# Key and query products of a chunk from float16 parts, and the gate's multiplication on VectorE

## The chip, the cores and the metric

The kernel runs on one core of a Trainium2 chip. Its engines are TensorE (PE in the rows; its weight loads stand apart as PEld), VectorE (DVE), ScalarE (ACT), GpSimd (POOL) and SyncE (SP, which issues the DMAs). Each works through its own queue of instructions in order, and they wait for one another by semaphores. The metric is the time on the device in microseconds (us), the median of several runs.

## The reference

A macaron block over x of shape (8, 512, 256): half a gated feed-forward network (width 768, quantised weights), a gated linear attention with the delta rule (16 heads of 128), and the same half network again. What matters here is the attention of one head:

```python
q = silu(conv(x @ Wq)); k = silu(conv(x @ Wk)) * D ** (-0.5); v = silu(conv(x @ Wv))
alpha = sigmoid(x @ Wa + ba); beta = sigmoid(x @ Wb + bb)
def step(St, inp):                       # one token
    err = St @ k_ - v_
    Sn = a_ * St - b_ * err[..., None] * k_[..., None, :]
    return Sn, Sn @ q_
o = layernorm(o) * ln_w + ln_b
g = sigmoid(x @ Wg)
return (o * g) @ Wo
```

conv is a causal convolution of four taps in each channel.

## The kernel before

**Tiling.** The 16 heads are taken in four groups of U = 4, and for each group the 8 sequences one after the other: 32 pairs of group and sequence (SEQ). A sequence of 512 tokens is cut into NC = 4 chunks of C = 128. So there are 128 chunks (STEPS), numbered t = 4n + c for pair n and chunk c. The token recurrence of a chunk is solved in matrix form: two products of the chunk, keys by keys (gram_k) and keys by queries (gram_q), each times a matrix of decays; the inverse of a triangular matrix, built in six levels (level_a and level_b on TensorE, each followed by a copy on VectorE or ScalarE); a solution and its correction; and the update of the state.

**Storage.** The rows of k, q and v (kb, qb, vb) and of the gate (gb) are float32 in SBUF, channels on partitions, twice for alternate pairs n. Weights and normed inputs are pairs of float16, high and low part, and the products of such pairs are made of three matmuls (high by high, high by low, low by high). The two chunk products take float32 operands straight from kb and qb: one call for each of four heads, which stands in the trace as two instructions.

**Where the projections lie.** While chunk t is solved, the projections for the next pair of group and sequence are made: project(t', j) with t' = 4n + i makes head j of k, q, v or gate for i = 0, 1, 2, 3, so each chunk's time holds one of the four. For i = 0, 1, 2 ScalarE starts the convolution (acc, L2219), VectorE does three taps for each head (tap, L1684) and ScalarE the silu (L2229). For i = 3 ScalarE applies tanh (gate, L2243), and there are no taps. Two PSUM banks take the projections in turn, and project(t', j) waits until the bank's last reader is done (tile_done).

**The output of a chunk.** statistics and aggregated (VectorE), root (POOL), normed (ScalarE), out_turned (TensorE), affine into oa (ScalarE), gated on POOL (oa times gb), high (ScalarE, the float16 part), low (POOL, the rest), output (TensorE, 12 matmuls) and the addition to the stream (VectorE). The gate is tanh plus 1 (the half is put in later): POOL adds the 1 in `one`, four instructions of 128x512 for each pair n.

**Order.** Each engine's block has a function step(s) that holds its order by hand for one chunk's time, a loop over it for the chunks of the middle, and orders written out line by line before and after. SyncE loads the decay and cumulative rows of each chunk and, at a change of the head group, the group's five weight pairs (load_pairs); the output weights wo16 have two places in SBUF, taken alternately.

**Two inputs in SBUF.** Of VectorE's instructions in the loop only the scan in decays (L1584) reads both inputs from SBUF. The others have at least one in PSUM.

## Time and profile before

| | |
|---|---|
| time, median of 3 runs | 2388.95 us (2388.93 to 2389.35) |
| the profiled execution's own time | 2389.32 us |
| its span, first to last instruction | 2387.6 us |
| mean granted TensorE clock | 0.996 |
| busy: PE, DVE, ACT, POOL | 98%, 85%, 76%, 76% |
| DMA | 43 GB/s on average |

Busy time of an engine is the time in which at least one of its instructions is in flight. TensorE's matmuls are pipelined: the duration of one holds the way through the array, in which the next has already started, so what an instruction costs a full TensorE is the distance between starts. For VectorE in a dense row, too, the next start lies about 0.08 us before the last end. Times in the timelines are microseconds from the span's start.

### The profile page before, as it was taken

The page shows a single profiled execution, that of the slowest core. Times are in us where ns is not written, and L with a number is a line of the kernel's source. Part 1 is how long each engine was busy: PE and PEld are TensorE (multiplying, and loading weights), DVE is VectorE, ACT ScalarE, POOL GpSimd, SP SyncE. Part 2 cuts the span into 40 slices and gives each one's busy share as a digit, 9 for nine tenths or more (in the row PEclk, how much of TensorE's full clock was granted, in tenths as well). Part 3 has the DMA queues.
Part 4 walks back from the last instruction along what each step waited for, and adds up shares of the span by engine and source line. Part 5 has one row for each costly group of instructions (what it writes and reads, how often), then busy time and mean ns, then how long its engine had stood idle before and what let it go on. Part 6 is the DMA issues. An engine that isn't in the chain of part 4 may idle for free. (4 is left out here: it accounts for less than half of the span.)

```text
span 2387.6 us, 64265 instructions
## 1 busy us (share of the span) xinstructions
PE 2338.4 (98%) x24496; PEld 1818.2 (76%) x24496; DVE 2023.1 (85%) x4282; ACT 1813.6 (76%) x3572; POOL 1809.2 (76%) x1936
## 2 busy tenths in 40 slices
PE   5999999999999999999999999999999999999998
PEld 2555778888888888788888887888888887887765
DVE  8788988888888888888889888888888888899653
ACT  3876777777777787777777877777777777788664
POOL 4774777877777777777777778777777777788775
PEclk8999999999999999999999999999999999999999
DMA  5450111111021111111121111111211121111001
GB/s 140 130 168 34 34 33 25 32 33 33 24 68 41 30 26 33 33 33 33 46 59 33 30 27 33 33 30 27 68 42 27 29 53 33 33 33 28 17 28 45
DMA packets 72832, 103.59 MB, mean 43 GB/s; under 512 B 21456, under 2 KB 33744, under 8 KB 72400
## 3 DMA queue, kind: packets, MB, share of 16 engines
q1 hardware_dynamic: 72528, 99.48, 16.3%
q8 instruction: 197, 3.23, 0.5%
q14 instruction: 107, 0.88, 0.1%
HBM read 85.69 MB, written 13.77 MB: 42 GB/s over the span
## 5 line engine op out<-in xcount | busy, mean ns | idle before, releaser
L1684 DVE SCALAR_TENSOR_TENSOR k_rows<-bank,k_prm,k_rows 128x511 f32<-128x511 f32 (+2 forms) x1152 | 842.5, 736 | 9.6 <-ACT k_rows L2219 8.8
L2970 PE MATMUL bank<-k_z,k_kqv 128*128 128x512 f16 x2304 | 597.4, 379 | 2.6 <-DVE k_rows L1684 2.5
L2281 ACT ACTIVATE k_wide<-bank 128x512 f16<-128x512 f32 x640 | 382.9, 599 | 200.3 <-PE bank L2803 184.5
L1613 DVE TENSOR_TENSOR k_y<-bank,k_masks 128x256 f16<-128x256 f32 x768 | 317.7, 414 | 120.5 <-PE bank L2789 116.6
L2219 ACT ACTIVATE k_rows<-bank,k_prm 128x512 f32<-128x512 f32 x384 | 299.4, 780 | 130.8 <-PE bank L2970 130.6
L2970 PEld LDWEIGHTS bank<-k_z,k_kqv 128*128 128x128 f16 x2304 | 197.5, 98 | 127.5 <-issue 4.7
L1205 POOL TENSOR_TENSOR k_diag<-k_ident,k_bcol 128x512 f32<-128x512 f32 x128 | 132.9, 1039 | 190.7 <-DVE a_prod L1584 190.6
L2803 PE MATMUL bank<-k_wide,k_y 128*128 128x64 f16 x3072 | 271.1, 192 | 0.0
L2789 PEld LDWEIGHTS bank<-k_wide 128*128 128x128 f16 x3072 | 169.0, 98 | 91.9 <-ACT k_wide L2281 1.8
L2801 PE MATMUL bank<-k_y,k_wide 128*128 128x64 f16 x2560 | 235.8, 193 | 2.7 <-DVE k_y L1613 0.8
L2803 PEld LDWEIGHTS bank<-k_wide,k_y 128*128 128x128 f16 x3072 | 207.0, 98 | 32.6
L2229 ACT ACTIVATE k_rows<-k_rows 128x512 f32<-128x512 f32 x384 | 230.3, 629 | 1.8 <-DVE k_rows L1684 1.8
L2801 PEld LDWEIGHTS bank<-k_y,k_wide 128*128 128x128 f16 x2560 | 196.8, 98 | 42.2 <-DVE k_y L1613 16.4
L1219 POOL TENSOR_TENSOR k_wide<-k_solve,k_ident 128x512 f16<-128x512 f32 x128 | 163.4, 1277 | 83.0 <-DVE k_solve L1593 78.6
L1301 POOL TENSOR_SCALAR k_rows<-k_rows 128x512 f32<-128x512 f32 x128 | 218.4, 1706 | 0.0
L2789 PE MATMUL bank<-k_wide 128*128 128x64 f16 x3072 | 215.1, 193 | 1.0 <-ACT k_wide L2281 0.7
L2970 PE MATMUL bank<-k_z,k_gate 128*128 128x512 f16 x768 | 201.4, 379 | 0.0
L2306 ACT ACTIVATE k_narrow<-bank,a_shift,a_rstd 128x128 f32<-128x128 f32 x512 | 191.7, 462 | 0.1
L2941 PE MATMUL bank<-k_wo,k_solve 128*128 128x256 f16 x1536 | 188.6, 273 | 0.0
L2901 PE MATMUL bank<-k_solve,k_wide 128*128 128x128 f32 x1024 | 184.9, 277 | 0.0
L1584 DVE TENSOR_TENSOR_SCAN a_prod<-a_decay,k_diag 128x516 f32<-128x516 f32 x128 | 180.3, 1408 | 0.5 <-ACT k_wide L2256 0.5
L1310 POOL TENSOR_TENSOR k_narrow<-k_narrow,k_rows 128x512 f32<-128x512 f32 x128 | 163.4, 1276 | 19.4 <-ACT k_narrow L2315 19.4
(158 smaller groups left out, 5870.2 us busy)
## 6 DMA issues: line engine op xcount, KB each, us to landing
a_decay<-decay_rows SPq DMA_DIRECT2D x128, 258.0 KB, 3.6
k_solve<-cumulative_rows SPq DMA_DIRECT2D x96, 258.0 KB, 3.6
weight_pairs<-k_wide SPq DMA_DIRECT2D x15, 512.0 KB, 2.9
k_kqv<-weight_pairs SPq DMA_DIRECT2D x9, 512.0 KB, 5.0
stream<-in_L_attn_x SPq DMA_DIRECT2D x8, 512.0 KB, 7.6
out<-stream SPq DMA_DIRECT2D x8, 512.0 KB, 2.9
k_rows<-in_L_attn_Wk SPq DMA_DIRECT2D x4, 512.0 KB, 4.7
k_rows<-in_L_attn_Wq SPq DMA_DIRECT2D x4, 512.0 KB, 5.2
```

The costliest lines, as they stand in the source:

```text
L1301: nc.gpsimd.tensor_scalar(gb[:, n % 2, j], gb[:, n % 2, j], 1.0, None, ALU.add).then_inc(m["pool_one"], 1)
L1613: nc.vector.tensor_tensor(even(y16[:, j], mb), bank[LEV[par]][:, 0:U * C // 2].rearrange("p (u b m) -> p u b m", u=U, m=mb), masks[:, j].r ...
L1684: nc.vector.scalar_tensor_tensor(out=dst[:, d:S], in0=bank[PJ[j % 2]][:, 0:S - d], scalar=prm[:, i, U * (n // B) + j, TAPS - 1 - d:TAPS - ...
L2219: nc.scalar.activation((kb, qb, vb)[i][:, n % 2, j], bank[PJ[j % 2]][:, :], ACT.Identity, bias=prm[:, i, h, TAPS:], scale=prm[:, i, h, TAP ...
L2229: nc.scalar.activation(dst, dst, ACT.Silu).then_inc(m[f"act_silu{j}"], 1)
L2281: nc.scalar.activation(both, bank[LEV[par]][:, :].rearrange("p (two b m) -> p two b m", two=2, m=mb), ACT.Copy).then_inc(m[f"act_lev{par}" ...
L2306: ins = nc.scalar.activation(on[:, u], bank[OUT][:, u * D:(u + 1) * D], ACT.Identity, bias=shift[:, u:u + 1], scale=rstd[:, u:u + 1])
L2789: mm = pe.matmul(at_half(LEV[par], 0, u), am16[:, par, u], halves(t16[par][:, u], mb, 0), start=True, stop=True)
L2801: pe.matmul(at_half(LEV[par], 0, u), tt16[par][:, u], halves(y16[:, j, u], mb, 0), start=True, stop=True)
L2803: mm = pe.matmul(at_half(LEV[par], half, u), y16[:, j, u], halves(tt16[par][:, u], mb, 1), start=True, stop=True)
L2941: mm = pe.matmul(bank[SUM][:, 0:H], o[:, u], wo16[:, group % WO_SLOTS, wh, u], start=(u == 0 and wh == 0 and o is oh), stop=(u == U - 1 an ...
L2970: mm = pe.matmul(bank[PJ[j % 2]][:, :], wt, z16[:, zh, k, cols], start=(x == 0), stop=(x == 5))
```

## The change

- A new tile k16 and a new tile q16 hold the float16 high part and low part of the keys and of the queries of one chunk. ScalarE makes the high parts (key_high, query_high: copies to float16), POOL the low parts (key_low, query_low: the row minus its high part, to float16).
- gram_k and gram_q make each head's product of three float16 matmuls of the parts (pair_products) instead of a float32 one.
- gated moves from POOL to VectorE and becomes one scalar_tensor_tensor, (gb + 1) * oa. `one` is gone.
- wo16 has one place instead of two. Its load at a change of the group comes three chunk times later and waits until the output of the last group's last chunk is done.
- pool_shift and pool_root (with their like) are one semaphore each.
- In the last block the second half of the last sequence is added to the stream by VectorE and stored by a DMA of its own. The down product of that block signals its first half early.
- step(s) of TensorE, VectorE, ScalarE and POOL is written in another order, and so are the written-out parts ahead of and behind the loops. Each engine still does all the same other work.

```diff
+    k16 = sb("k16", [P, 2, U, C], F16); q16 = sb("q16", [P, 2, U, C], F16)
...
@@ SyncE
-            group, kind = divmod(s - NC * (B - 1) + 2, NC * B)
+            group, place = divmod(s - NC * (B - 1) + 2, NC * B)
             group += 1
-            if kind >= KINDS or not 0 < group < HG:
+            kind = KINDS - 1 if place == WO_PLACE else place
+            if not 0 < group < HG or kind >= KINDS or place == KINDS - 1:
                 return
...
-                need(sp, m["pe_wo"], NC * B * (group - WO_SLOTS + 1))
+                need(sp, m["pe_wo"], NC * B * group)
...
@@ POOL
-        def one(t, j):
...
-            pool.wait_ge(m[f"act_gate{j}"], n + 1)
-            nc.gpsimd.tensor_scalar(gb[:, n % 2, j], gb[:, n % 2, j], 1.0, None, ALU.add).then_inc(m["pool_one"], 1)
...
-            nc.gpsimd.tensor_tensor(oa[:, :, :], oa[:, :, :], gb[:, n % 2, :, c * C:(c + 1) * C],
-                                    ALU.mult).then_inc(m["pool_og"], 1)
+        def key_low(t):
...
+            pool.wait_ge(m["act_kh"], t + 1)
+            nc.gpsimd.tensor_tensor(k16[:, 1], kb[:, n % 2, :, c * C:(c + 1) * C], k16[:, 0],
+                                    ALU.subtract).then_inc(m["pool_kl"], 1)
...
+            pool.wait_ge(m["act_qh"], t + 1)
+            nc.gpsimd.tensor_tensor(q16[:, 1], qb[:, n % 2, :, c * C:(c + 1) * C], q16[:, 0],
+                                    ALU.subtract).then_inc(m["pool_ql"], 1)
...
+            system16(s)
+            first_inverse(s)
+            query_low(s)
+            scaled_q(s - 1)
+            scaled_k(s - 1)
+            root(s - 2)
+            low(s - 3)
+            strengths(s + 1)
             system_low(s)
+            key_low(s + 1)
             state(s - 1)
...
@@ VectorE
+        def gated(t):
...
+            dve.wait_ge(m["act_oa"], t + 1)
+            if c == 0:
+                for j in range(U):
+                    dve.wait_ge(m[f"act_gate{j}"], n + 1)
+            nc.vector.scalar_tensor_tensor(out=oa[:, :, :], in0=gb[:, n % 2, :, c * C:(c + 1) * C], scalar=1.0,
+                                           in1=oa[:, :, :], op0=ALU.add, op1=ALU.mult).then_inc(m["dve_og"], 1)
...
+            level(s - 1, 3)
+            tap(s + 2, 0, 2)
+            gated(s - 3)
+            tap(s + 2, 0, 3)
+            tap(s + 2, 1, 1)
+            statistics(s - 2)
+            level(s - 1, 4)
...
+            level(s, 1)
+            tap(s + 2, 2, 2)
+            tap(s + 2, 3, 1)
+            tap(s + 2, 2, 3)
+            output(s - 3)
+            tap(s + 2, 3, 2)
+            decays(s + 1)
+            tap(s + 2, 3, 3)
+            residual(s - 1)
+            level(s, 2)
+            system(s + 1)
+            corrected(s - 1)
+            tap(s + 3, 0, 1)
...
+                nc.vector.tensor_tensor(rows, rows, scaled[:, 2:4], ALU.add).then_inc(f["dve_last"], 1)
...
@@ ScalarE
+        def key_high(t):
...
+            need(act, m["pe_gram0"], t)
+            need(act, m["pe_gram1"], t)
+            nc.scalar.activation(k16[:, 0], kb[:, n % 2, :, c * C:(c + 1) * C], ACT.Copy).then_inc(m["act_kh"], 1)
...
+            need(act, m["pe_gram1"], t)
+            nc.scalar.activation(q16[:, 0], qb[:, n % 2, :, c * C:(c + 1) * C], ACT.Copy).then_inc(m["act_qh"], 1)
...
+            level(s, 4)
+            key_high(s + 2)
+            level(s + 1, 0)
+            normed(s - 1)
+            acc(s + 3, 3)
...
@@ TensorE
+        def pair_products(dst, a, b, u):
+
+            pe.matmul(dst, a[:, 0, u], b[:, 0, u], start=True, stop=False)
+            pe.matmul(dst, a[:, 0, u], b[:, 1, u], start=False, stop=False)
+            return pe.matmul(dst, a[:, 1, u], b[:, 0, u], start=False, stop=True)
...
-                mm = pe.matmul(units(TURN)[:, u], kb[:, n % 2, u, cols], kb[:, n % 2, u, cols], start=True, stop=True)
+                mm = pair_products(units(TURN)[:, u], k16, k16, u)
...
-                mm = pe.matmul(units(TURN)[:, u], kb[:, n % 2, u, cols], qb[:, n % 2, u, cols], start=True, stop=True)
+                mm = pair_products(units(TURN)[:, u], k16, q16, u)
...
+            check_solution(s - 2)
+            project(s + 2, 0, 2)
+            gram_k(s)
+            project(s + 2, 1, 0)
+            correction(s - 2)
+            level_b(s - 1, 2)
...
```

## Rows read from the trace of the kernel before

**Rows 1.** The page: busy us of each engine, share of the span, instructions.

```profile
PE 2338.4 (98%) x24496; PEld 1818.2 (76%) x24496; DVE 2023.1 (85%) x4282; ACT 1813.6 (76%) x3572; POOL 1809.2 (76%) x1936
```

**Rows 2.** Stretches: us, busy PE, PEld, DVE, ACT, POOL (x instructions), clock, DMA.

```profile
1200.00:1600.00 400.00, 399.54 (x4456) 322.24 (x4455) 352.57 (x756) 314.72 (x630) 314.77 (x331) 1.00 0.13 34
...
1008.16:1057.71 49.55, 49.48 (x550) 40.16 (x549) 47.79 (x99) 38.56 (x76) 38.94 (x42) 1.00 0.14 34
1057.71:1071.65 13.94, 13.94 (x163) 10.94 (x163) 7.87 (x21) 11.36 (x24) 10.71 (x12) 1.00 0.08 20
```

**Rows 3.** Timeline of PE around one gram_k: start us, us in flight, engine, line.

```profile
1003.98 0.22 PE L2860 MATMUL bank<-k_solve,k_wide 128*128 128x128 f16 x1
...
1004.42 0.19 PE L2801 MATMUL bank<-k_y,k_wide 128*128 128x64 f16 x1
...
1004.66 1.14 PE L2739 MATMUL bank<-k_rows 128*128 128x128 f32 x8
1005.63 0.39 PE L2873 MATMUL bank<-k_solve,k_wide 128*128 128x128 f16 x4
1005.86 0.38 PE L2970 MATMUL bank<-k_z,k_kqv 128*128 128x512 f16 x1
```

**Rows 4.** Timeline of PE, the next gram_q.

```profile
1010.24 1.11 PE L2753 MATMUL bank<-k_rows 128*128 128x128 f32 x8
```

**Rows 5.** Timeline of DVE: the first tap of two successive pairs.

```profile
1008.16 0.75 DVE L1684 SCALAR_TENSOR_TENSOR k_rows<-bank,k_prm,k_rows 128x511 f32<-128x511 f32 x1 [0.27 <-ACT k_rows L2219]
...
1071.65 0.75 DVE L1684 SCALAR_TENSOR_TENSOR k_rows<-bank,k_prm,k_rows 128x511 f32<-128x511 f32 x1 [0.27 <-ACT k_rows L2219]
```

**Rows 6.** Timeline of DVE and of POOL around one scan, inside the taps.

```profile
1016.69 0.74 DVE L1684 SCALAR_TENSOR_TENSOR k_rows<-bank,k_prm,k_rows 128x511 f32<-128x511 f32 x1
1017.35 2.06 DVE L1584 TENSOR_TENSOR_SCAN a_prod<-a_decay,k_diag 128x516 f32<-128x516 f32 x1
...
1017.27 1.05 POOL L1280 TENSOR_TENSOR k_narrow<-k_narrow,k_solve 128x512 f32<-128x512 f32 x1
1018.29 2.40 POOL L1301 TENSOR_SCALAR k_rows<-k_rows 128x512 f32<-128x512 f32 x1
```

**Rows 7.** DVE: group of L1584 (busy us, mean ns), then lines with ns min/median/max.

```profile
L1584 DVE TENSOR_TENSOR_SCAN a_prod<-a_decay,k_diag 128x516 f32<-128x516 f32 x128 | 180.3, 1408 | 0.5 <-ACT k_wide L2256 0.5
...
L1584 DVE TENSOR_TENSOR_SCAN a_prod<-a_decay,k_diag x128: 1195/1223/2061, 180.9 to 2224.2; 128x516 f32<-128x516 f32 x128
...
L502 DVE SCALAR_TENSOR_TENSOR k_kqv<-k_rows,k_kqv x3: 1215/1216/1985, 63.5 to 82.0; 128x1024 f16<-128x1024 f32 x3
...
L515 DVE TENSOR_TENSOR k_rows<-k_rows x9: 693/693/1684, 7.7 to 49.0; 128x512 f32<-128x512 f32 x9
```

**Rows 8.** Groups of ACT and POOL by line.

```profile
L2323 ACT ACTIVATE k_solve<-k_narrow 128x512 f16<-128x512 f32 x128 | 79.2, 619 | 1.0 <-POOL k_narrow L1310 1.0
...
L1301 POOL TENSOR_SCALAR k_rows<-k_rows 128x512 f32<-128x512 f32 x128 | 218.4, 1706 | 0.0
L1310 POOL TENSOR_TENSOR k_narrow<-k_narrow,k_rows 128x512 f32<-128x512 f32 x128 | 163.4, 1276 | 19.4 <-ACT k_narrow L2315 19.4
L1241 POOL TENSOR_TENSOR k_wide<-k_solve,k_wide 128x512 f16<-128x512 f32 x128 | 148.3, 1159 | 0.1
```

**Rows 9.** Waits of the whole span: us in total, times, longest us.

```profile
POOL k_diag L1205 <- DVE a_prod L1584: 190.6, 93, 9.5
...
PEld bank L2860 <- ACT k_solve L2298: 25.6, 124, 0.5
...
PEld bank L2801 <- DVE k_y L1613: 16.4, 65, 0.7
```

**Rows 10.** Timeline of the end: the last scaling and the last additions.

```profile
2380.93 1.29 DVE L1770 TENSOR_TENSOR k_rows<-bank,k_rows 128x512 f32<-128x512 f32 x2 [4.49 <-PE bank L3078]
2381.70 2.48 POOL L1366 TENSOR_TENSOR stream<-stream,k_rows 128x512 f32<-128x512 f32 x2 [2.40 <-DVE k_rows L1770]
```

**Rows 11.** DMA issues: count, KB each, median us to landing.

```profile
k_wo<-weight_pairs SPq DMA_DIRECT2D x3, 512.0 KB, 5.6
```

More of the change, by code:

```diff
@@ L1894, in _ @@
         tap(4, 2, 2)
+        level(1, 5)
         level(2, 1)
@@ L2566, in _ @@
         level(5, 4)
+        key_high(7)
         level(6, 0)
-        acc(8, 2)
+        normed(4)
+        acc(8, 3)
+        right_side(5)
+        level(5, 5)
         kdecayed(6)
-        normed(4)
-        level(5, 5)
-        right_side(5)
         level(6, 1)
```

1878 lines of the change are left out of this document (1110 added, 768 removed).

## Prediction, made before the changed kernel was run

> **What bounds the kernel now.** I read the page's busy shares first: TensorE is busy for 98% of the span, VectorE for 85% [rows 1]. Such a share is an average, so the next view is the table of stretches. In 400 us of the middle TensorE has work in flight for 399.54 us at the full clock (1.00, the level of 2.4 GHz) [rows 2]. So in the loop every instruction taken from TensorE shortens the time, until another engine ends last. Of the 49 us that TensorE is idle in the span (2387.6 - 2338.4 [rows 1]) only some 2 us can lie in the loop (0.46 us in 400); the rest is at the two ends.
>
> The pattern repeats once for each pair of heads' group and sequence, which is four chunks: the first tap of a pair starts at 1008.16 and that of the next at 1071.65, so a period is 63.49 us [rows 5]. 32 periods are 2032 us of the 2387.6 us of span. Inside a period VectorE's load is uneven. The three chunks whose projections are keys, queries and values have 12 taps each, the fourth none. From the first tap to the last (1008.16 to 1057.71) VectorE is busy for 47.79 of 49.55 us; in the other 13.94 us it is busy for 7.87 us [rows 2]. I call the 49.55 us the tap stretch. In it VectorE is nearly as full as TensorE, which the share of 85% hides. This decides the case.
>
> **TensorE's part.** A float32 product of four heads is 8 instructions. The keys' product starts at 1004.66 and the next work at 1005.63: 0.97 us [rows 3]. The keys by queries are in flight for 1.11 us [rows 4]; less the same tail as above (1.14 - 0.97 = 0.17) that is 0.94 us. I take distances between starts, since the time in flight holds the way through the array, where the neighbour overlaps. The new product is 12 float16 matmuls of the same 128x128 shape. Eight such with changing weights take 1004.42 - 1003.98 = 0.44 us, or 55 ns each; four others 1005.86 - 1005.63 = 0.23 us, or 57 ns [rows 3]. Twelve are 0.66 to 0.69 us; I take 0.67. A chunk saves 0.97 + 0.94 - 2 * 0.67 = 0.57 us, a period 2.3 us, 128 chunks 73 us. The low parts accumulate in the same place of PSUM, as the projections do.
>
> One rule speaks against this. The Trainium skill, TensorE: Matmul & The Clock Gate, section Back-to-back issue gap, says that in a real stream of weight loads and matmuls the spacing at 128 columns is about 81 ns. By it twelve would take 0.97 us (estimate from the page), nothing would be saved, and the time would be 2389 us or more. The 55 ns here are from such a stream with a new weight load for each matmul, so the trace disagrees.
>
> **VectorE's part.** It gets one instruction of 128x512 for each chunk with both inputs in SBUF. The nearest rows: an addition of that shape takes 693 ns, and the same operation over 1024 elements 1216 ns [rows 7]. In a dense queue the next start comes 0.08 us before the end (a tap of 0.74 us starts at 1016.69, the scan at 1017.35 [rows 6]), so it costs 0.60 us in the queue; as bounds, 0.53 us (half of 1216 less 0.08) and 0.69.
>
> On top comes what the other input from SBUF does. The scan is the only such instruction now. Its median is 1223 ns and its longest 2061 [rows 7]: at 1017.35 it starts while POOL is in an instruction that ends at 1018.32, and lasts 0.84 us longer than the median; POOL's next lasts 2.40 us, 0.9 more than it would alone [rows 6]. They exclude each other. This happens to about one scan of four (mean 1408, median 1223 [rows 7]: 0.19 us a scan, 0.74 us a period). Most scans are spared because POOL sits waiting for that very scan: 190.6 us in all [rows 9]. In the new order POOL has strengths further from the scan it waits for, and gated comes two to three instructions after system, on whose end POOL starts system16 and first_inverse. So collisions are possible for three scans and three gated in a tap stretch. Bounds: none, or 0.84 us each, 5.0 us a period. If VectorE met POOL by chance, at its share of 38.94 in 49.55 us [rows 2] and half of some 1.1 us left, it would be 0.43 us each, 2.6 us. I take 1.3 us a period, 0.5 more than now, since POOL's long `one` is gone and its next idle time begins before system16.
>
> The Trainium skill, SBUF — State Buffer, has the rule for this: a VectorE instruction with two SBUF inputs and a GpSimd instruction that reads SBUF block each other for the whole instruction. The trace agrees with 2061 against 1223 ns.
>
> Now the sum for a tap stretch. TensorE's share of it falls by three chunks, 1.7 us, to 47.8 us. VectorE's real idle time is 49.55 - 47.79 = 1.76 us, plus the 0.08 us of overlap that each of its some eight short gaps would give back, 2.4 us. So its load is 47.1 us (with one collision), and with three gated 48.9, with 0.5 of further collisions 49.4. It exceeds TensorE's time by 1.6 us. TensorE can wait out some of that, since a level's copy may come late: I estimate 0.3 us, from PE's weight loads that already sit idle for VectorE's copy 65 times for 16.4 us in total, 0.25 us each [rows 9]. Give-back: 1.3 us a period. Net: 2.3 - 1.3 = 1.0 us a period, 32 us in all.
>
> **ScalarE and POOL.** ScalarE gets two copies of 0.62 us a chunk [rows 8], 3.7 us in the tap stretch: 38.56 + 3.7 = 42.3 of 47.8 us [rows 2], 88%. It costs nothing as long as level copies are not late behind them; if that cover is gone, a late copy costs TensorE what the queue holds, 0.6 us. For the solution's copy TensorE's weight loads wait already in 124 chunks, 0.2 us each [rows 9], so cover is thin. key_high waits for the previous chunk's gram_q; behind it in ScalarE's queue stand level, normed and acc, and for level waits TensorE. POOL loses 1.71 us (`one`) and 1.28 (gated) a chunk and gains two subtractions of 1.16 to 1.28 us [rows 8]: 0.4 to 0.7 us less. New chain: silu, high, low, product. At the first chunk of a pair it is 1.8 us longer (0.62 + 1.16) and gram_k waits on POOL; behind gram_k stand correction and level_b. gram_q now comes later in the step and has cover. gated waits for ScalarE's affine; behind it in VectorE's queue stand taps and level copies; affine is a good part of a chunk earlier in ScalarE's order, so nothing.
>
> **Queues and ends.** The output weights' load comes at three group changes on SP, behind the cumulative and decay loads of its step and ahead of the next ones, and waits for the last group's output. It lands in 5.6 us [rows 11], and the first output that needs it comes a chunk, 15 us, later: nothing; 17 us in all if that were wrong. Merged semaphores: nothing. At the end POOL's two additions run from 2381.70 to 2384.18 [rows 10]; with the second on VectorE, 0.6 us after its scaling that ends at 2382.22 and some 0.2 us earlier from the early signal, the last store starts about 1.7 us sooner. The rewritten beginning may move TensorE's idle time there by 4 us either way (estimate, a tenth of the 49 us).
>
> **Rivals.**
> - *TensorE alone bounds.* If the tap stretch has more slack than I count, all is kept: 2389 - 73 - 2 = 2314 us. For: TensorE's 399.54 of 400. Against: 47.79 of 49.55.
> - *Nearly all is given back*, by ScalarE's thin cover or collisions at the chance rate (2.6 us a period instead of 0.8: give-back 1.1 + 1.8 - 0.3 = 2.6 us, net -0.3; half of that excess gives +0.3 to +0.6 us): 2370 to 2390 us, 2380 in the middle.
> - *Slower: collisions on VectorE in the tap stretch.* With six of 0.5 us instead of one of 0.84 the give-back is 1.1 + 2.2 - 0.3 = 3.0 us against 2.3 saved: 32 * 0.7 = 22 us more, 2409 us. It decides from 2.3 us of collisions a period. For: the exclusion is in the trace. Against: POOL's idle share, and its own wait chains that fall together with VectorE's.
> - *The product isn't cheaper.* In the tap stretch TensorE starts 550 matmuls in 49.55 us, 90 ns apart on average [rows 2]. At 80 ns twelve cost what the float32 product costs and nothing is saved, 2389 us; at 90 ns each of 256 products costs 0.12 us more, 2420 us; 2400 in between. Against: 55 ns with changing weights [rows 3]. The Trainium skill's 81 ns (above) would be this rival.
>
> **How the numbers follow.** The profiled execution took 2389.32 us with a span of 2387.6, and the median of the runs is 2388.95, so they may be exchanged. Forecast: 2388.95 - 32 - 2 = 2355 us. Chances: forecast (2333 to 2370) 0.53; TensorE alone (2308 to 2332) 0.18; nearly all given back 0.15, half of it within 0.2%; slower by collisions 0.10; product not cheaper 0.04. A measurement of this kernel can tell about 0.2%, or 5 us, from no change. Faster: 0.53 + 0.18 + 0.07 = 0.78; within 0.2%: 0.08 + 0.02 = 0.10; slower 0.12. The range from 2314 to 2386 us leaves out the upper cases and a little of TensorE alone.
>
> **What would show it.** The products' distance in the timeline should be 0.66 to 0.69 us. The period should be 62.5 us. VectorE should be dense in the tap stretch, over 98%, with TensorE idle or its weight loads waiting for k_y, k_solve and k_rows of VectorE; if TensorE stays at 399.5 of 400 us and the period is 61.2, the first rival is right. The scan's and gated's medians against their longest durations give the collisions. Wrong would be: a f16 spacing over 70 ns, ScalarE as the named releaser of TensorE's new idle time, or a stall at the three group changes.

## The result, and the profile after

| | before | after |
|---|---|---|
| time, median of 4 runs each, side by side | 2389.15 us | 2408.41 us (2407.91 to 2408.60) |
| ratio | | 1.008, 95% interval 1.0067 to 1.0093 |
| span of the profiled execution | 2387.6 us | 2406.2 us |

The changed kernel is 19 us slower. The forecast was 2355 us with a range that ended at 2386, so both its sign and its range were wrong.

The page of after: busy us, share of the span and instructions; then the chain that ended last.

```profile
PE 2341.1 (97%) x25520; PEld 1730.8 (72%) x25520; DVE 2107.0 (88%) x4411; ACT 1967.4 (82%) x3828; POOL 1773.9 (74%) x1935
...
PE 67%; DVE 25%; issue 4%; POOL 2%; ACT 1%; DMA 0%; DVEq 0%; SPq 0%; POOLq 0%; ACTq 0%
```

TensorE's busy time is what it was [rows 1], 2341 against 2338 us, though it has 73 us less to do. A quarter of the chain now lies on VectorE.

Stretches of after, columns as in [rows 2]: first the middle, then the tap stretch of one period and its rest. To compare kernels I cut both at starts of taps: from a period's first tap to the start of its last one, and from there to the next period's first tap.

```profile
1200.00:1600.00 400.00, 396.49 (x4614) 300.52 (x4612) 360.58 (x764) 340.62 (x673) 301.48 (x325) 1.00 0.13 34
...
1016.02:1063.16 47.14, 46.63 (x534) 35.29 (x532) 46.82 (x98) 39.89 (x78) 37.98 (x41) 1.00 0.10 24
1063.16:1080.22 17.06, 17.06 (x212) 13.05 (x210) 11.33 (x28) 14.90 (x32) 10.41 (x12) 1.00 0.17 48
```

The kernel before, by the same cuts:

```profile
1008.16:1056.97 48.81, 48.74 (x544) 39.42 (x543) 47.05 (x98) 38.34 (x76) 38.28 (x41) 1.00 0.14 34
1056.97:1071.65 14.68, 14.68 (x170) 11.68 (x169) 8.61 (x22) 11.58 (x25) 11.38 (x13) 1.00 0.08 19
```

A period went from 63.49 to 47.14 + 17.06 = 64.20 us; 32 times 0.71 is 23 us, so the two ends gave some 4 us back. VectorE is busy for 46.82 of 47.14 us of the tap stretch, 99.3% (96.4% before). The rest of the period belongs to TensorE alone in both kernels. The granted clock is 1.00, the full one, in all of these stretches.

The product itself: TensorE in after, one gram_k and what follows it.

```profile
1030.25 0.22 PE L2900 MATMUL bank<-a_k 128*128 128x128 f16 x1
1030.30 0.22 PE L2901 MATMUL bank<-a_k 128*128 128x128 f16 x1
...
1030.92 0.59 PE L3154 MATMUL bank<-k_z,k_kqv 128*128 128x512 f16 x2
```

Twelve matmuls take 1030.92 - 1030.25 = 0.67 us. That was the forecast to the hundredth.

VectorE's instructions with two inputs in SBUF in after: ns min/median/max of the scan (L1597) and of gated (L1693), the groups' busy us and mean ns, and one gated beside POOL's queue.

```profile
L1597 DVE TENSOR_TENSOR_SCAN a_prod<-a_decay,k_diag x128: 1220/1416/2175, 204.4 to 2246.5; 128x516 f32<-128x516 f32 x128
...
L1597 DVE TENSOR_TENSOR_SCAN a_prod<-a_decay,k_diag 128x516 f32<-128x516 f32 x128 | 182.8, 1428 | 6.3 <-ACT k_wide L2327 6.1 <-POOL k_diag L1212 0.2
...
L1693 DVE SCALAR_TENSOR_TENSOR k_narrow<-k_rows,k_narrow x128: 658/956/1477, 263.1 to 2296.8; 128x512 f32<-128x512 f32 x128
...
L1693 DVE SCALAR_TENSOR_TENSOR k_narrow<-k_rows,k_narrow 128x512 f32<-128x512 f32 x128 | 115.6, 903 | 0.3 <-ACT k_narrow L2386 0.3
...
1034.33 0.98 DVE L1693 SCALAR_TENSOR_TENSOR k_narrow<-k_rows,k_narrow 128x512 f32<-128x512 f32 x1
...
1033.60 1.17 POOL L1238 TENSOR_TENSOR k_wide<-k_wide,k_mask0t 128x512 f16<-128x512 f16 x1
1034.72 1.61 POOL L1317 TENSOR_TENSOR a_q<-k_rows,a_q 128x512 f16<-128x512 f32 x1
```

gated starts at 1034.33 while POOL is in L1238 until 1034.77, and takes 0.98 us; with one input in PSUM it takes 0.68 (below). POOL's next takes 1.61 us. The median scan, 1223 ns before [rows 7], is 1416. Per period both together lose 4 * (903 - 676) + 4 * (1428 - 1223) ns = 1.7 us to POOL, against 0.74 before.

The waits of after (us in total, times, longest us):

```profile
PEld bank L2985 <- DVE k_y L1626: 55.4, 157, 1.1
PEld bank L2973 <- ACT k_wide L2352: 48.1, 155, 0.5
PEld bank L3034 <- issue: 43.8, 119, 0.4
PEld bank L3013 <- issue: 36.8, 86, 0.4
PEld bank L3057 <- DVE k_solve L1636: 23.3, 62, 0.7
PEld bank L3154 <- DVE k_rows L1708: 21.5, 52, 0.8
...
PE bank L3154 <- DVE k_rows L1708: 15.5, 41, 1.9
```

Of before there were two such lines in the loop, 25.6 and 16.4 us [rows 9]. Two of the new ones name no engine ("issue"): weight loads ahead of first_solution (L3034) and state_k (L3013). The weight loader idles while the array still holds earlier work, so a busy TensorE doesn't show it: in the kernel with the new order and the old work (below) TensorE is in flight for all but 0.14 us of a period, and the waits ahead of first_solution are 43 us all the same.

Where the order costs distances: `read` in before, then in after, then first_solution in after.

```profile
1023.34 0.47 PE L2900 MATMUL bank<-k_narrow 128*128 128x128 f32 x2
1023.64 0.39 PE L2901 MATMUL bank<-k_solve,k_wide 128*128 128x128 f32 x2
1023.86 0.39 PE L2900 MATMUL bank<-k_narrow 128*128 128x128 f32 x2
```

```profile
1033.03 0.46 PE L3084 MATMUL bank<-k_narrow 128*128 128x128 f32 x2
1033.32 0.39 PE L3085 MATMUL bank<-k_solve,k_wide 128*128 128x128 f32 x2
1033.54 0.39 PE L3084 MATMUL bank<-k_narrow 128*128 128x128 f32 x2
...
1034.22 0.47 PE L3084 MATMUL bank<-k_narrow 128*128 128x128 f32 x2
1034.53 0.39 PE L3085 MATMUL bank<-k_solve,k_wide 128*128 128x128 f32 x2
...
1027.62 0.59 PE L3154 MATMUL bank<-k_z,k_kqv 128*128 128x512 f16 x2
1028.16 0.38 PE L3034 MATMUL bank<-k_solve,k_wide 128*128 128x128 f16 x4
```

The first pair of float32 matmuls behind float16 work takes 0.30 us to the next start, the later ones 0.22. `read` is now in two halves with level_b between them, so that 0.08 us is paid twice a chunk. Two projection matmuls ahead of first_solution take 0.54 us; elsewhere two take 0.43 (1029.82 to 1030.25 in the same kernel).

### The profile page after: what moved, and what is told of

The parts are those of the page before. It is cut to its first block, busy times and chain, and to the rows that moved or that the text cites. A ratio compares the mean times of both kernels' runs of the same rounds, so it can differ in the third digit from the quotient of the medians.

```text
span 2406.2 us, 67114 instructions
## 1 busy us (share of the span) xinstructions
PE 2341.1 (97%) x25520; PEld 1730.8 (72%) x25520; DVE 2107.0 (88%) x4411; ACT 1967.4 (82%) x3828; POOL 1773.9 (74%) x1935
## 3 DMA queue, kind: packets, MB, share of 16 engines
q1 hardware_dynamic: 72544, 99.48, 16.4%
## 4 chain that ended last, share of the span: by engine, by line
PE 67%; DVE 25%; issue 4%; POOL 2%; ACT 1%; DMA 0%; DVEq 0%; SPq 0%; POOLq 0%; ACTq 0%
PE bank L3154 20%; DVE k_rows L1708 11%; PE bank L3125 5%; PE bank L3224 3%; PE bank L3084 3%; PE bank L3013 3%; DVE k_y L1626 3%; PE bank L2973 3%; PE bank L3085 2%; PE bank L2985 2%; PE bank L2987 2%; PE bank L828 2%; PE bank L3102 2%; PE bank L2900 2%; PE bank L3003 2%
## 5 line engine op out<-in xcount | busy, mean ns | idle before, releaser
L1708 DVE SCALAR_TENSOR_TENSOR k_rows<-bank,k_prm,k_rows 128x511 f32<-128x511 f32 (+2 forms) x1152 | 814.5, 732 | 1.2 <-ACT k_rows L2267 0.6
L3154 PE MATMUL bank<-k_z,k_kqv 128*128 128x512 f16 x2304 | 637.0, 380 | 18.8 <-DVE k_rows L1708 15.5
L2973 PEld LDWEIGHTS bank<-k_wide 128*128 128x128 f16 x3072 | 167.6, 97 | 129.8 <-ACT k_wide L2352 48.1
L3154 PEld LDWEIGHTS bank<-k_z,k_kqv 128*128 128x128 f16 x2304 | 179.3, 98 | 108.7 <-DVE k_rows L1708 21.5
L2985 PEld LDWEIGHTS bank<-k_y,k_wide 128*128 128x128 f16 x2560 | 188.7, 97 | 63.5 <-DVE k_y L1626 55.4
L3154 PE MATMUL bank<-k_z,k_gate 128*128 128x512 f16 x768 | 212.0, 379 | 0.1
L2987 PEld LDWEIGHTS bank<-k_wide,k_y 128*128 128x128 f16 x3072 | 197.8, 98 | 8.3
L1317 POOL TENSOR_TENSOR a_q<-k_rows,a_q 128x512 f16<-128x512 f32 x128 | 189.2, 1478 | 7.3 <-ACT a_q L2315 7.3
L3085 PE MATMUL bank<-k_solve,k_wide 128*128 128x128 f32 x1024 | 192.2, 280 | 0.0
L1597 DVE TENSOR_TENSOR_SCAN a_prod<-a_decay,k_diag 128x516 f32<-128x516 f32 x128 | 182.8, 1428 | 6.3 <-ACT k_wide L2327 6.1
L1238 POOL TENSOR_TENSOR k_wide<-k_wide,k_mask0t 128x512 f16<-128x512 f16 x128 | 163.4, 1276 | 10.1 <-PE bank L3057 0.3
L3084 PE MATMUL bank<-k_narrow 128*128 128x128 f32 x768 | 162.9, 294 | 0.2
```

The lines of the kernel that those rows point to most:

```text
L1708: nc.vector.scalar_tensor_tensor(out=dst[:, d:S], in0=bank[PJ[j % 2]][:, 0:S - d], scalar=prm[:, i, U * (n // B) + j, TAPS - 1 - d:TAPS - ...
L2973: mm = pe.matmul(at_half(LEV[par], 0, u), am16[:, par, u], halves(t16[par][:, u], mb, 0), start=True, stop=True)
L2985: pe.matmul(at_half(LEV[par], 0, u), tt16[par][:, u], halves(y16[:, j, u], mb, 0), start=True, stop=True)
L2987: mm = pe.matmul(at_half(LEV[par], half, u), y16[:, j, u], halves(tt16[par][:, u], mb, 1), start=True, stop=True)
L3084: pe.matmul(units(OUT)[:, u], qg[:, u], z[:, u], start=True, stop=False)
L3085: mm = pe.matmul(units(OUT)[:, u], mix[:, t % 2, u], wv[:, u], start=not c, stop=True)
```

## The experiments

Each ratio is against the kernel before on the same chip, whose median was 2389.2 to 2389.6 us in every group.

**The gate's instruction made short.**

```diff
-  ...scalar_tensor_tensor(out=oa[:, :, :], in0=gb[..., c * C:(c + 1) * C], scalar=1.0, in1=oa[:, :, :], ...)
+  ...scalar_tensor_tensor(out=oa[:, :, 0:4], in0=gb[..., c * C:c * C + 4], scalar=1.0, in1=oa[:, :, 0:4], ...)
```

> The changed kernel with gated on VectorE cut to 4 of 128 columns of each head (the rest of the gate's multiplication is left out). Theory A: VectorE's load binds the three chunks with taps (50.0 us from one first tap to where the next pair's would be), so without 0.50 us of work and about 0.28 us of collision for each of three chunks the stretch falls to TensorE's 47.5 us and the period from 64.2 to about 61.9 us: 2335 us. Theory B: the new order of TensorE's own queue leaves gaps whatever VectorE does: 2395 us or more. Theory C: ScalarE's two added copies are late: 2395 us or more.

2370.78 us (ratio 0.9922, 0.9907 to 0.9937): the instruction at full size costs 37.6 us more than the short one. None of the three theories had this: the first expected 2335 us, the others 2395 or more. VectorE is 99% busy in the tap stretch even so (45.44 of 45.95 us):

```profile
1002.72:1048.67 45.95, 45.68 (x534) 35.34 (x532) 45.44 (x98) 39.02 (x78) 36.61 (x41) 1.00 0.11 25
1048.67:1065.72 17.05, 17.05 (x212) 13.05 (x210) 10.80 (x27) 14.90 (x32) 9.93 (x12) 1.00 0.17 48
```

TensorE waits less for VectorE in it:

```profile
PEld bank L2985 <- DVE k_y L1626: 29.8, 98, 1.1
...
PEld bank L3154 <- DVE k_rows L1708: 6.6, 23, 0.8
```

In the changed kernel these two lines are 55.4 and 21.5 us. By distances from start to start, 0.5 of the 1.2 us a period that the full size costs lies between `update` and the projection behind it (L3154), whose PSUM bank VectorE's taps (L1708) still read; the rest is spread over several places.

**The products as before, in float32.**

```diff
-  mm = pair_products(units(TURN)[:, u], k16, k16, u)
+  mm = pe.matmul(units(TURN)[:, u], kb[..., cols], kb[..., cols], start=True, stop=True)
```

(and the same for keys by queries)

> The changed kernel with both chunk products made again from float32 rows; parts are still made and not used. TensorE gets 2.3 us a period back. Theory A: in the stretch with taps VectorE ends last, so only the fourth chunk pays its 0.57 us: 18 us more than the changed kernel, 2427 us. Theory B: TensorE's queue is the limit everywhere, gaps included: 73 us more, 2481 us.

2434.94 us (1.0190, 1.0175 to 1.0206): inside the changed kernel the float16 products bring 26.5 us, not the 73 of their distances. That is nearer to theory A's 2427 us than to theory B's 2481.

**The gate's second input from a bank at rest** in the three chunks with taps; the output of those chunks is multiplied with other data.

```diff
-  in1=oa[:, :, :]
+  in1=bank[PJ[0]][:, :]... if (s + 2) % NC < NC - 1 else oa[:, :, :]
```

> The changed kernel, but in chunks with taps gated takes its second input from a PSUM bank that lies still instead of from oa (the result is another). One input in SBUF: it should no longer collide with POOL. Theory A with collisions: 0.25 to 0.3 us less in each of three chunks, 0.06 us more for the PSUM input: about 0.6 us a period, 20 us less: 2388 us. Rival: collisions cost nothing, 2408 us.

2378.10 us (0.9954, 0.9939 to 0.9969). Same size, same place, one input in PSUM: 30.3 us back, half as much again as theory A's 20. gated falls from 903 to 676 ns:

```profile
L1694 DVE SCALAR_TENSOR_TENSOR k_narrow<-k_rows,bank 128x512 f32<-128x512 f32 x86 | 58.1, 676 | 0.0
L1694 DVE SCALAR_TENSOR_TENSOR k_narrow<-k_rows,k_narrow 128x512 f32<-128x512 f32 x42 | 32.4, 771 | 0.3 <-ACT k_narrow L2387 0.3
```

So most of the 37.6 us are collisions with POOL, not the instruction's own length. (Collisions are the cases in which an instruction of VectorE with both inputs in SBUF and one of POOL hold each other up.)

**The gate back on POOL** in the new order, with the 1 added on VectorE in the light chunk.

```diff
-  dve: scalar_tensor_tensor(oa, gb, 1.0, oa, ADD, MULT)
+  pool: gated_to(t - 3) ahead of system16: tensor_tensor(oa, oa, gb, MULT)
+  dve: one(n, j), tensor_scalar(gb[:, n % 2, j], ..., 1.0, ALU.add), in the chunk without taps
```

> Float16 products kept; the multiplication by the gate back on POOL (in its idle time ahead of system16), the added 1 on VectorE as four instructions of 128x512 in the chunk without taps. Theory A: VectorE's stretch is as in the kernel before, TensorE binds again with 2.3 us less: 2335 to 2350 us. Theory B or C: 2395 us or more. If POOL becomes late (1.28 us more a chunk) system16 comes later and TensorE's first_inverse waits: 2370 us.

2458.20 us (1.0289, 1.0272 to 1.0306). The last of the mechanisms that I had written, POOL late, is the one that the waits show, but I had priced it at 2370 us. POOL waits for ScalarE's affine ahead of system16 and is late with everything behind it:

```profile
POOL k_narrow L1312 <- ACT k_narrow L2413: 132.6, 117, 3.2
...
PEld bank L3084 <- DVE k_solve L1654: 89.8, 89, 2.2
```

It tells nothing of VectorE's load.

**One part or both in the order of before.** Three kernels: the gate on VectorE ahead of the level copy j = 3; the parts alone; both.

```diff
 level(t, j), VectorE
+            if j == 3:
+                gated_to(t - 2)
```

> The kernel before, in its own order, with one part of the change: the instruction (gb + 1) * oa on VectorE ahead of the level copy j = 3, and neither `one` nor the multiplication on POOL. The products stay float32. Nothing is left out of the computation. Theory L (VectorE's load and its collisions with POOL are what the change loses): VectorE gains four instructions of 0.60 us in a period, in the tap stretch three, where it has some 2 us of idle time; the previous runs put the gate's instruction at 38 us in the new order, where the stretch was fuller, because TensorE was shorter there. With TensorE still at its old length I expect 2389 to 2415 us, 2400 in the middle. Rival O (the new order of the engines costs, not VectorE): within 5 us of the kernel before, 2389 us.

2489.22 us (1.0420, 1.0404 to 1.0435). A miss, far above both ranges. gated takes 1147 ns on average here, against 659 at the least:

```profile
L1532 DVE SCALAR_TENSOR_TENSOR k_narrow<-k_rows,k_narrow 128x512 f32<-128x512 f32 x128 | 146.9, 1147 | 0.0
```

So some 62 of its 147 us are collisions, and the rest is its own length; the scan collides less than before (1226 ns on average). VectorE's busy time in the span grew by 2133.5 - 2023.1 = 110 us, the time by 100. The instruction stands ahead of a level copy in this order, and how much of the 100 us is that place wasn't told apart.

```diff
 order of before, with ScalarE and POOL (and VectorE's mixing moved, wo16 with one place)
+    high copies (act_kh, act_qh) ahead of level(t, 0) and kdecayed; key_low behind system_low, query_low behind first_inverse
+    gram_q behind level_a(t, 0); k_turned behind level_b(t, 0)
```

> The kernel before with the other part alone: both chunk products from float16 parts, with ScalarE's and POOL's instructions for them; the gating stays on POOL with `one`. The order is that of before, save for two products (keys by queries stands behind level_a of the level 0, the turned keys behind level_b of it), VectorE's mixing, and the place of the output weights. Nothing is left out. POOL now has everything of before and two subtractions of 1.2 us a chunk: its 314.77 us busy in 400 become 314.77 + 25.2 x 2.4 = 375, 94%. Theory L: TensorE's 73 us come through as far as POOL isn't late: 2320 to 2345 us. Rival P (POOL is late, as when the gating was put on it in the new order): 2370 us or more, with TensorE and VectorE waiting for POOL.

2672.78 us (1.1188, 1.1172 to 1.1205), rival P, and far beyond the 2370 that it named. POOL waits for ScalarE's query_high, and ScalarE for POOL's shift:

```profile
POOL a_q L1219 <- ACT a_q L2234: 273.0, 127, 4.9
...
ACT k_narrow L2365 <- POOL a_shift L1322: 231.3, 125, 2.3
```

> Both parts in the order of before: products from float16 parts, gating on VectorE, `one` gone. It is the whole change but for the rewritten order. Nothing is left out. Theory L (VectorE's load alone is the loss): the load is the same as in the changed kernel, so the time is too, 2400 to 2415 us. Rival O (the new order costs 1.2 us a period or more on TensorE, as the gaps that are left when the gate's instruction is made short suggest): 2408 less 38 = 2370 us, below 2380 at any rate.

2702.69 us (1.1312, 1.1293 to 1.1331), outside both ranges. These last two show only that the parts need places of their own in ScalarE's and POOL's queues, not what the order of the changed kernel costs. The next ones ask that from the other side.

**The new order with the old work**: float32 products and the gate's instruction on 4 columns, which is the first two edits together. It leaves out most of the gate, on POOL too, which has neither `one` nor the multiplication.

> The changed kernel with neither of its two effects: the products are float32 calls again (the parts are still made by ScalarE and POOL) and the gate's instruction on VectorE works on 4 of 128 columns, which leaves most of the gate out of the output. So TensorE has the work of the kernel before, VectorE too (but 0.1 us a chunk), and what differs is the order. If the effects add up: 2370.8 + (2434.9 - 2408.4) = 2397 us. Rival O (order costs of its own): 2397 us or more against 2389 for the kernel before. Theory L (the order costs nothing, its gaps are VectorE's): within 5 us of 2389.

2411.09 us (1.0091, 1.0076 to 1.0106). Rival O, and more than the 2397 us that the sum of the effects gives: TensorE's work is as before, and the kernel is 22 us slower.

**The same with the parts' four instructions on 4 columns.**

```diff
-  activation(k16[:, 0], kb[..., c * C:(c + 1) * C], ACT.Copy)
+  activation(k16[:, 0, :, 0:w], kb[..., c * C:c * C + w], ACT.Copy)    # w = C if t < 2 else 4
```

(and likewise query_high, key_low, query_low)

> The new order with the old work (float32 products, the gate's instruction on 4 of 128 columns), and now ScalarE's and POOL's four instructions for the parts on 4 of 128 columns too, from the third chunk on. Most of the gate is left out; the parts feed nothing. What is left of the change is the order of the queues. Theory T (the order of TensorE itself costs): the time stays at 2411 us, within 5. Rival S (the load of ScalarE and POOL, 2.4 and 4.8 us in a chunk's time of 16, makes copies late): back to 2389 to 2395 us.

2408.82 us (1.0081, 1.0066 to 1.0096). ScalarE's and POOL's added work is 2.3 us of the 22; 19.5 are left. They are not the price of the order by itself, since the gate's short instruction is still in VectorE's queue and takes far more than the 0.1 us that I had counted, 570 ns on average:

```profile
L1695 DVE SCALAR_TENSOR_TENSOR k_narrow<-k_rows,k_narrow x128: 142/417/1109, 264.4 to 2297.6; 128x16 f32<-128x16 f32 x128
```

That is 73 us of busy time which VectorE doesn't have in the kernel before, and no run takes it out. The period:

```profile
1018.13:1064.46 46.33, 46.19 (x514) 37.02 (x512) 45.48 (x98) 37.02 (x78) 31.17 (x41) 1.00 0.10 25
1064.46:1082.24 17.78, 17.78 (x200) 13.94 (x198) 11.67 (x27) 14.17 (x32) 8.06 (x12) 1.00 0.16 46
```

64.11 us, 0.62 more than before, with TensorE in flight for all but 0.14 us. VectorE is full in the tap stretch here too, 98%: the new order packs the same taps in 46.33 instead of 48.81 us. Three of the short instructions, 3 * (0.57 - 0.08) = 1.5 us, are among the 45.48.

**Two places of TensorE's order put back**, in the changed kernel and in the one with the old work.

```diff
-            read(s - 2, 0, U // 2)
-            level_b(s - 1, 3)
-            read(s - 2, U // 2, U)
+            read(s - 2, 0, U // 2)
+            read(s - 2, U // 2, U)
+            level_b(s - 1, 3)
...
-            first_solution(s - 1)
-            out_turned(s - 2)
+            out_turned(s - 2)
+            first_solution(s - 1)
```

> The changed kernel with two places of TensorE's order in the loop put as they were before: the two halves of `read` stand together again ahead of level_b(s - 1, 3), and out_turned stands ahead of first_solution. Nothing is left out. Reason: the kernel with the new order and the old work takes 2411 us against 2389, and in its rows the distances between starts are longer at read (0.6 us a period above that of its matmuls, 0.3 before), behind the first half of read (0.2) and ahead of first_solution (0.3; 43.8 us of weight loads that wait for nothing shown, none before). Theory O (these places are the cost of the order): 0.6 to 0.8 us a period come back as far as TensorE bounds; VectorE is full in the tap stretch, so about half of it: 2393 to 2403 us. Rival L (VectorE alone holds the stretch): within 5 us of 2408.

2434.77 us (1.0190, 1.0175 to 1.0206).

> The same two places in the kernel with the new order and the old work (float32 products, the gate's instruction on 4 of 128 columns, which leaves most of the gate out), where TensorE is in flight for 399.0 of 400 us and nothing else presses. Theory O: 0.6 to 0.8 us a period, 19 to 26 us, come back: 2385 to 2392 us, which is the time of the kernel before. Rival G (the gaps only move to the next place, since what the weight loads wait for lies elsewhere): 2405 us or more.

2450.74 us (1.0258, 1.0242 to 1.0273). The first misses both of its ranges; the second is rival G, and far above its 2405. The weight loads of first_solution no longer wait, but those of check_solution (L3046) do, on ScalarE's copy of the solution, and those of level_a (L2975) wait 83.1 us for ScalarE, 62.2 in the kernel with the new order and the old work. The lines are of the second kernel:

```profile
PEld bank L2975 <- ACT k_wide L2352: 83.1, 267, 0.8
PEld bank L3046 <- ACT k_solve L2369: 30.1, 116, 0.3
```

The wait's total understates it: by distances between TensorE's starts in the kernel with the old work, `read` and first_solution gave back the 0.8 to 0.9 us a period that I had wanted, while level_a to check_solution lost 1.2, and `update` and a projection to what follows them another 0.4 each.

**The halves alone**, in the changed kernel (the first three lines of the edit above).

> The changed kernel with the two halves of `read` together ahead of level_b(s - 1, 3), and nothing else moved; nothing is left out. In the kernel with two places moved the distances at read fell by 0.3 us a period and behind its first half by 0.2. Theory T: 0.5 us a period where TensorE bounds, up to 16 us: 2393 to 2403 us. Rival: level_b comes 0.6 us later in each chunk, VectorE's and ScalarE's copies of the levels with it, and the chain of levels then costs more: 2408 to 2420 us.

2420.17 us (1.0128, 1.0113 to 1.0143), the upper end of the rival. level_b later by half a `read` costs more than the 0.08 us that the second half's start behind float16 work costs.

**The parts small in the changed kernel.**

> The changed kernel with the four instructions for the parts on 4 of 128 columns from the third chunk on, so the products take the parts of early chunks for most columns and the output is another. TensorE and VectorE have the whole work of the changed kernel. POOL gets free earlier, so collisions fall as well. Theory T with VectorE full: within 10 us of 2408. Rival S (ScalarE's and POOL's added work holds up the copies): 2380 us or less.

2387.82 us (0.9993, 0.9983 to 1.0003): 20.6 us back, between the two ranges. The scan is free of collisions in it, gated isn't (888 ns):

```profile
L1599 DVE TENSOR_TENSOR_SCAN a_prod<-a_decay,k_diag 128x516 f32<-128x516 f32 x128 | 158.2, 1236 | 6.6 <-ACT k_wide L2331 6.4 <-POOL k_diag L1212 0.2
```

VectorE's scans fell by 182.8 - 158.2 = 24.6 us. The same edit was worth 2.3 us with the gate's short instruction and float32 products. Whether ScalarE's lighter queue has a share stayed open here.

**The scan out of POOL's way**, all work kept, nothing but two VectorE instructions exchanged.

```diff
-            decays(s + 1)
             tap(s + 2, 3, 3)
+            decays(s + 1)
```

> The changed kernel with decays(s + 1) and tap(s + 2, 3, 3) exchanged on VectorE, and nothing else; nothing is left out. The scan then starts some 0.65 us later, when POOL's `state` is over (in the rows the scan starts at 1028.59 and POOL's `state` ends at 1028.91). Theory C (VectorE's length in the tap stretch is the path, and collisions of the scan are part of it): the scan's mean falls to 1220 to 1280 ns, and 15 to 24 us come back: 2385 to 2394 us. Rival S (the 20.6 us of the run with small parts came from ScalarE's lighter queue): 2403 us or more, whatever the scan's duration.

2396.86 us (1.0032, 1.0019 to 1.0045). The median scan is 1224 ns again, the mean 1281; 18.8 us less busy, 11.5 us less time. A bit short of what theory C wanted, clearly off the rival's 2403. So of the 20.6 us above some 12 can be called shown for collisions; the other 9 may be ScalarE's or POOL's.

```profile
L1597 DVE TENSOR_TENSOR_SCAN a_prod<-a_decay,k_diag 128x516 f32<-128x516 f32 x128 | 164.0, 1281 | 6.6 <-ACT k_wide L2327 6.4 <-POOL k_diag L1212 0.2
```

**Neither collides**: the exchange, and the gate's second input from the bank at rest.

> The same exchange, and the gate's instruction takes its second input from a bank at rest in the chunks with taps, so that the gate's factor is multiplied with other data; VectorE then has no two-input instruction from SBUF near POOL's work. Theory C: the two gains add up as far as VectorE is the path. Without the gate's collisions the time was 2378; the scan's mean was 1315 there, so 10 us of busy time are left to take, and TensorE is near its bound: 2368 to 2375 us. Rival S: 2378, unchanged.

2377.24 us (0.9950, 0.9935 to 0.9965), no different from 2378.10 without the exchange. This is rival S's number, though not its reason: once gated is out of POOL's way the scan's collisions cost nothing, and something else ends last at 2377.

**The gate early, in POOL's idle time.**

```diff
             decays(s + 1)
+            gated(s - 2)
             tap(s + 2, 3, 3)
             residual(s - 1)
...
-            gated(s - 3)      # in the next step
```

> The changed kernel with gated a half chunk's time earlier on VectorE: gated(s - 2) right behind decays(s + 1), where POOL sits idle for 3.3 us ahead of system16, instead of behind the first tap of the next step, where POOL is in first_inverse or query_low. Nothing is left out. Theory C: gated's durations fall to 0.68 us and some 0.3 us each comes back, 0.9 to 1.2 us a period with the tap behind it; residual and system come 0.6 us later. 2375 to 2395 us. Rival (what is behind it now, residual and corrected, is on the path of the next chunk, and its delay eats the gain): 2400 us or more with gated at 0.68 us all the same.

2433.83 us (1.0186, 1.0171 to 1.0201), the rival. gated is down to 708 ns, and correction's weight loads wait for residual, behind which it now stands, for 49.1 us instead of 23.3:

```profile
L1696 DVE SCALAR_TENSOR_TENSOR k_narrow<-k_rows,k_narrow 128x512 f32<-128x512 f32 x128 | 90.6, 708 | 10.5 <-ACT k_narrow L2390 8.5
...
PEld bank L3061 <- DVE k_solve L1636: 49.1, 118, 0.6
```

**The gate through PSUM, nothing left out.** affine writes into the bank OUT, gated reads it there, `read` waits for gated of the chunk ahead.

```diff
-  nc.scalar.activation(oa[:, :, :], units(TURN), ACT.Identity, ...)
+  nc.scalar.activation(units(OUT) if t < STEPS - 3 else oa[:, :, :], units(TURN), ACT.Identity, ...)
 gated (the wait for POOL's low, from ScalarE's affine):
+  need(dve, m["pool_ol"], t)
 read:
+  need(pe, m["dve_og"], min(t, STEPS - 3))
```

> The changed kernel with one input of the gate's instruction in PSUM, and the output right: ScalarE's affine writes its result into the bank OUT, which is free between normed and the next read, and the gate's instruction reads it there and writes oa. `read` now waits for the gate's instruction of the chunk ahead; the last three chunks keep the old way. Nothing is left out. Theory C (collisions of two inputs from SBUF with POOL are some 30 us of the 38 that the instruction costs): 2378 us, as when the input came from a bank at rest; with the new wait of read up to 2385. Rival (the instruction's length counts, not its port): 2400 us or more.

2646.97 us (1.1079, 1.1063 to 1.1096). gated takes 677 ns, and each `read` waits some 2 us for it, because it stands behind a level copy and a tap:

```profile
PEld bank L3087 <- issue: 180.4, 91, 3.7
PE bank L3087 <- DVE k_narrow L1694: 171.9, 91, 3.6
```

> The gate through PSUM and the two places of TensorE's order together, nothing left out. If both causes are real and apart: 2378 less 19 to 26 us, 2352 to 2365 us, faster than the kernel before. If only the collisions are real: 2378. If neither: 2400 or more.

2723.90 us (1.1401, 1.1382 to 1.1420). Both are misses; the rival's "2400 us or more" holds as a number, but not its reason, since 677 ns show that the collisions are gone. They have one lesson: I had priced the wait from when affine is done, not from where gated stands in its queue. No version that does all the work beat the kernel before; the nearest was the exchange of scan and tap, 0.3% slower.

## Why the prediction was wrong, point by point

The runs make a chain from one kernel to the other, one thing changed at a time:

| step | us | difference | period, us |
|---|---|---|---|
| before | 2389.3 | | 63.49 |
| new order with the old work (the gate's instruction short) | 2408.8 | +19.5 | 64.11 |
| + ScalarE's and POOL's instructions for the parts | 2411.1 | +2.3 | 64.14 |
| + float16 products | 2370.8 | -40.3 | 63.00 |
| + gated on VectorE at full size = after | 2408.4 | +37.6 | 64.20 |

The prices hold for this sequence of steps. With float32 products the full-size gate costs 2434.9 - 2411.1 = 23.8 us instead of 37.6, and with the full-size gate the float16 products bring 26.5 instead of 40.3.

**The product's price was right**, 0.67 us against 0.66 to 0.69. The rule of the page TensorE: Matmul & The Clock Gate of the Trainium skill (section Back-to-back issue gap), 81 ns at 128 columns, is contradicted here by 56 ns over twelve matmuls with a new weight load each (1030.25 to 1030.92).

**First step that failed: the order cost nothing.** The sum had no term for it. With the old work it is 19.5 us, together with whatever the gate's short instruction costs there and POOL's lighter queue gives back; these shares weren't measured. I read "each engine still does all the same other work" as "TensorE needs the same time for it", but distances depend on what stands next to what: `read` in two halves, and weight loads that wait ahead of first_solution for 43.8 us in total, where before had no such line. From the starts of all of TensorE's instructions of one period, taken one by one and set against 216 ns for a projection matmul, 111 for a float32 one and so on, I get 1.4 us a period above those in before and 2.1 in the new order with the old work, which accounts for the period's 0.62. The larger parts are `read` from its first to its last start, 0.3 us more, from its first half to level_b 0.2, and from a projection to first_solution 0.3. These are the order's and not VectorE's: with the two places put back they went away. But they are not a slip of the order either: taken back, they come again elsewhere and cost more. So why an order without them isn't to be had stays open.

**Second step: what the saving is worth before anything is given back.** I let TensorE's three chunks in the tap stretch count until VectorE's load, 47.1 us with one collision, was reached, and gave back only what gated adds. But in the new order the tap stretch is 46.3 us long and VectorE fills 98% of it before the products become cheaper, the gate's short instruction included. The float16 products then shorten the tap stretch by 46.35 - 45.95 = 0.40 us, and the rest of the period by 17.79 - 17.05 = 0.74 us; that is 1.14 of the 2.06 us that the products' distances fell by (7.45 us a period as float32 in that order, 5.39 now, both added up from start to start; 7.72 in the kernel before). The kernel with the old work and the parts at full size, for the 46.35:

```profile
1019.19:1065.54 46.35, 46.21 (x514) 37.00 (x512) 45.70 (x99) 39.21 (x78) 36.65 (x41) 1.00 0.11 25
1065.54:1083.33 17.79, 17.79 (x200) 13.94 (x198) 11.68 (x28) 14.97 (x32) 9.95 (x12) 1.00 0.15 46
```

The profile's page said 85% for VectorE and the tap stretch 96%. I saw that and called the other 1.76 us idle time that could be filled; the new order had already used it.

**Third: the size of the give-back.** Forecast for gated and its collisions: 1.3 us a period. Measured: 1.20 (37.6 us). That agrees only by its total, since the parts differ. Of own length I had 1.8 us a period in the tap stretch, 1.1 of it above TensorE's time, and for collisions 0.5 more. By the run with the bank at rest, the length beyond a short instruction is worth 2378.1 - 2370.8 = 7.3 us in all (at least, since the short one still collides), and collisions 30.3 (with those of the scan: its group fell from 182.8 to 168.3 us there). Collisions are 1.7 us of VectorE's time a period, not the 1.3 I took nor the 2.6 of the chance rate. The median scan is hit now, since POOL's `state` is still running at the scan's start (it ends at 1028.91, the scan starts at 1028.59); I had said that most scans are spared because POOL sits waiting for that scan. In the new order it no longer waits for it: POOL's long wait is for `system`.

**The rivals.** "Slower by collisions" forecast 2409 us, and the time is 2408.4. The agreement of the number is luck. Its mechanism is real, but its sum was not: it wanted 3.0 us of collisions a period and decided from 2.3; there are 1.7. Without the 19.5 us of the new order, which no rival had, the gate's 37.6 would have ended at no change, if the prices add up (2.3 - 40.3 + 37.6). "TensorE alone" fell with 99.3%. "The product isn't cheaper" fell with 0.67 us.

**The smaller terms.** ScalarE as the releaser of TensorE's new idle time was named as a sign that the forecast would be wrong, and it is there (48.1 us of weight-load waits for level copies against 25.6 for the solution's before); with the parts small it is not less (65.6 us in 211 waits), so it isn't the parts that make it. POOL at 74% has spare time and still sets VectorE's length. The two ends gave 4 us where I had 2.

**What stays open.** The time without collisions is 2377 us, and with the gate's instruction nearly gone 2371. TensorE is in flight for 398.4 and 398.8 of 400 us there, so waits are few, but its distances are longer than its work. How much of that is in TensorE's order and how much in copies that come just late wasn't told apart, and neither was ScalarE's share in the 20.6 us of the small parts. What the new order costs without any instruction of the gate on VectorE wasn't run.

## What to carry to other kernels

When a second engine is nearly full in a stretch (96 to 99% here), price a change by that stretch alone: cheaper TensorE work is worth its full price only outside it. A new order is a term of the sum of its own even where all the work is the same; build it with the old work first, all of it and nothing more, to see what it costs. And an instruction with two inputs in SBUF has no fixed price on VectorE: look at what POOL is doing at the moment it would start.

## What the runs showed of the hardware

- The collision price depends on place and hardly on size. gated at 128x512 takes 676 ns with one input in PSUM, 708 in POOL's idle time, 903 in the changed kernel and 1147 in the order of before. Made 32 times smaller it still takes 444 ns in the median and 946 at most, since it waits for POOL's instruction:

```profile
L1693 DVE SCALAR_TENSOR_TENSOR k_narrow<-k_rows,k_narrow x128: 144/444/946, 263.7 to 2259.4; 128x16 f32<-128x16 f32 x128
```

This is the rule of the Trainium skill, SBUF — State Buffer (section SBUF: two separate sides): whichever starts first holds the pair of ports for its whole instruction. The runs agree. They also show the part that matters here: the mean lies above the shortest by 903 - 658 = 245 ns at full size and by 387 - 144 = 243 ns for the short one, so a short instruction pays the same as a long one.

- A group of float32 matmuls behind float16 ones has a first distance of 0.30 us for two, then 0.22. Splitting such a group, or putting a short float16 group inside it, costs 0.08 us each time.
- In the stretches where VectorE is dense, a microsecond less of its busy time was worth 0.6 us (scan behind the tap: 11.5 of 18.8), 0.77 (gate from a bank at rest: 30.3 of 298.4 - 258.8 = 39.6) and, in the order of before, 0.9 (100 of 110, as a cost). From the short gate to the full-size one out of POOL's way it was only 0.3 (7.3 of 24.7, VectorE's busy 2047.9 against 2072.6), since the time is then near what something else allows.
